# A vision-transformer layer on one core: where the odd group's attention weights are turned, where the even gates stand, and who issues the transfers that place the weights

## Chip, cores and metric

One core of one Trainium2 chip runs the whole kernel as a single program. The metric is the device time of one execution in microseconds (us). The kernel before has been timed three times; the median is given below.

## What is computed

64 images of 3x96x96 are cut into 36 patches of 16x16x3; each is multiplied to 256 features, a class token is put in front (37 tokens per image) and position vectors are added. Then follow one attention layer over the 37 tokens of each image (16 heads of 64) and one mixture-of-experts layer (8 experts, top 2, beside a shared one), each with a residual and a layer norm. The unusual part of attention is the position term, taken from a running sum of gates:

```python
sim = jnp.einsum('bid,bjd->bij', q, k) * scale
G = jax.nn.sigmoid(sim)
P = jnp.flip(jnp.cumsum(jnp.flip(G, axis=-1), axis=-1), axis=-1)
P = jnp.minimum(P, T_MAX - 1)
E = jnp.einsum('bnc,ct->bnt', q, pos_emb)
w = P - floor(P)
sim = sim + w * E[ceil(P)] + (1.0 - w) * E[floor(P)]
attn = jax.nn.softmax(sim, axis=-1)
out = jnp.einsum('bij,bjd->bid', attn, v)
```

All of it is in fp32.

## The kernel before

The work of the attention layer goes by **groups** of three images (111 rows, `ROWS`) and by **pairs** of groups. Group `g = 2p + a` is the even (`a = 0`) or odd (`a = 1`) group of pair `p`; there are 22 groups and 11 pairs, 0 to 10. The last group has one image and a packed form of its own. Pair 0 is written out (`first_pair` on TensorE and ScalarE), pairs 1 and 10 are written out too, and pairs 2 to 9 run in loops (on ScalarE 2 to 8, and 9 behind them). After attention come the shared expert, the router and the routed experts; the change doesn't touch them.

Nothing is scheduled by a tool: each engine's instructions stand in the order in which its block is written, and semaphores couple the engines. For one group the steps are these.

- `score(p, a)` on TensorE (L1010) gives scores and the products with the position table for all heads, in six PSUM banks `S`. VectorE copies the table part of an even group out (`tables_out`, L1985); ScalarE copies the scores out in three overlapping copies (L1494, L1496, L1498). ScalarE waits for VectorE's copy before it starts its own, and counts up `sim_sb` when the third is done. For an odd group ScalarE copies the table too (L1505).
- `values(p, a, s)` on TensorE (L1025, two products of 512 columns in four matmuls per two halves `k`) gives half `s` of the values in a bank of `X`; ScalarE's `values` (L1529) copies it out and counts up `v_ready`. Group `a = 1` uses the same two banks as `a = 0`, so TensorE's `values(p, 1, s)` waits until half `s` of the even group has been copied.
- ScalarE's `gates(p, a)` (tanh at L1514, then the gate at L1516) starts VectorE's long chain `cope`: the running sum `u` (L1908), its nearest even number and remainder (L1912, L1915), five bit masks (L1917), five predicated copies (L1925), the look-up (L1929 to L1942), and the logits (L1945 to L1949). In its midst (before L1933) it needs `qpos` from ScalarE's `distance` (L1523, L1524).
- ScalarE's `softmax_exp` (L1567) and VectorE's `softmax_norm` (L1969, L1971, L1975) give the attention weights `attn`.
- `turn_weights` on TensorE (L1047, eight transposes) turns them into two of the score banks. It waits for the next group's scores to be out of `S` (`sim_sb`, `table_sb`) and for the weights themselves (`attn_ready`). ScalarE's `weights` (L1535) copies them out, and six DMA transfers of 46 KB (`to_diagonal(j, b)`, two halves `j` by three images `b`) put the blocks on the diagonal of `attnT`. SyncE issues them (`place_attn`, L647). For group 0 and for groups 19 and 20, ScalarE issues the three of half `j = 1` behind its copies (L1546); `in_two_queues` says which.
- `outputs(g, a)` on TensorE (L1065) waits for all six (`placed`), and ScalarE copies the result to `oT` (L1559). `residual` (L1074) and `by_tokens` (L1090) finish a pair one pair later; `embed`, `keys` and `queries` (L921, L930) feed the next one.

In the loop, TensorE's order for pair `p` is: queries of `p` with the outputs of group `2p-2` between them, score of group `2p`, its two halves of values, **turn_weights of group 2p-1**, both halves of values of group `2p+1`, embed of the next pair, outputs of `2p-1`, score of `2p+1`, residual of the pair before, first keys, **turn_weights of group 2p**, keys, by_tokens. ScalarE's order from the scores on is:

```python
score(p, 0)
values(p, 0, 0)
values(p, 0, 1)
weights(p * 2 - 1, 1)
gates(p, 0)
split(p - 2)
distance(p * 2)
halves_of_x(p + 2)
outputs(p * 2 - 1, 1)
```

`split` prepares the normed rows of two pairs ago and `halves_of_x` the pixels of two pairs ahead. SyncE, in its own queue, goes through: store the hidden state, store normed rows, place the odd group (six issues), store halves, load pixels, turn pixels by a DMA transpose, place the even group (six issues), load the hidden state back.

Of the kernel before, what the change touches and what calls it, by code (L numbers as in the profile page):

```python
# [15 lines left out]
def vit_tower(nc, x, tok_w, tok_b, cls_token, pos_embed, wq, wkv, wout, b_out, cope_emb,  # L16
# [17 lines left out]
    TPG = 3  # L34
    ROWS = TPG * TOK
    G = -(-IMGS // TPG)
# [46 lines left out]
    with ExitStack() as ctx:  # L83
# [252 lines left out]
        o_done = sem("o_done")  # L336
# [108 lines left out]
        def to_diagonal(j, b):  # L445

            return (own_T[PAD * b:PAD * b + PAD, b, j * BLOCKS:j * BLOCKS + BLOCKS],
                    turned_attn[PAD * j:PAD * j + PAD, b])

        def in_two_queues(g):  # L450

            return isinstance(g, int) and (g == 0 or g >= G - 3)

        def slot_of(h):

# [16 lines left out]
        def next_first(p):  # L472
            return isinstance(p, int) and p == 1
# [50 lines left out]
        def apart(eng):  # L524

            eng.nop(nofuse=True)
# [56 lines left out]
        def _(sp):  # L583
# [52 lines left out]
            def place_attn(p, a):  # L636

                g = p * 2 + a
                if first(g):
                    sp.wait_ge(attnT_zeroed, 1)  # L640
                else:
                    sp.wait_ge(o_done, g * 2)
                sp.wait_ge(at_sb, g * 4 + 4)
                apart(sp)
                for j in range(2 - in_two_queues(g)):
                    for b in range(TPG):
                        sp.dma_start(*to_diagonal(j, b)).then_inc(placed[a], 16)  # L647

            def turn_x(p):

# [245 lines left out]
        def _(pe):  # L896
# [311 lines left out]
            def pair(p, ahead):  # L1208
# [8 lines left out]
                else:  # L1217
                    queries(p, ahead)
                    score(p, 0)
                    for s in range(2):  # L1220
                        values(p, 0, s)
                if ahead:
                    turn_weights(p * 2 - 1, True)
                    values(p, 1, 0)
                else:
                    values(p, 1, 0)
                    turn_weights(p * 2 - 1, True)
                    for c in range(2):
                        turn(c)
                values(p, 1, 1)  # L1230
# [228 lines left out]
        def _(act):  # L1459
# [66 lines left out]
            def values(p, a, s):  # L1526
                act.wait_ge(v_done, p * 4 + 2 * a + s + 1)
                keyed = keys_of(rows_of(p * 2 + a))
                nc.scalar.copy(v_sb[:keyed, a, 512 * s:512 * s + 512], X[:keyed, 1 - s]  # L1529
                               ).then_inc(v_ready, 1)  # L1530

            def weights(g, a):
                for j in range(2):
                    act.wait_ge(at_done, g * 4 + 2 * j + 2)
                    nc.scalar.copy(turned_attn[:2 * PAD, :, PER_BANK * j:PER_BANK * j + PER_BANK],  # L1535
                                   S[:2 * PAD, j, :PER_BANK * ROWS].rearrange("p (n b q) -> p b n q", n=PER_BANK, b=TPG)
                                   ).then_inc(at_sb, 2)

                if in_two_queues(g):
                    if g == 0:  # L1540
                        act.wait_ge(attnT_zeroed, 1)
                    else:
                        act.wait_ge(o_done, g * 2)
                    act.wait_ge(at_sb, g * 4 + 4)
                    for b in range(TPG):
                        act.dma_start(*to_diagonal(1, b)).then_inc(placed[a], 16)  # L1546

            def packed_weights(j):
                r = rows_of(G - 1)
# [13 lines left out]
            def softmax_exp(g):  # L1563
                act.wait_ge(logits, g + 1)
                r = lanes(g)
                n = heads(r)
                nc.scalar.activation(ex[:r, :n], lg[:r, :n], ACT.Exp).then_inc(exp_ready, 1)  # L1567
# [84 lines left out]
            def pair(p, ahead, ahead2):  # L1652
# [14 lines left out]
                values(p, 0, 0)  # L1667
                if not ahead:
                    softmax_exp(p * 2 - 1)
                values(p, 0, 1)  # L1670
                if ahead:
                    weights(p * 2 - 1, 1)
                if not next_first(p):
                    gates(p, 0)
                    split(p - 2)
                if ahead:
                    distance(p * 2)
# [812 lines left out]
```

## Time and profile before

| what | value |
|---|---|
| median of 3 runs | 717.65 us (717.54 to 722.87) |
| the profiled execution | 716.74 us |
| its span, first to last instruction | 715.0 us |
| TensorE busy | 683.1 us, 96% of the span |
| VectorE busy | 489.1 us, 68% |
| ScalarE busy | 422.9 us, 59% |
| chain that ended last | PE 44%, DVE 34%, issue 9%, ACT 7%, DMA 4% |
| mean granted clock of TensorE | 0.994 of full speed |

In profile rows PE is TensorE, PEld its weight loads, DVE VectorE, ACT ScalarE, POOL GpSimd, and SPq and ACTq are the sequencers of SyncE and ScalarE when they issue a transfer. A row of the timeline gives the start and the length of a run of like instructions in us. Neighbouring groups on one engine overlap a little (a group's length includes the emptying of the pipeline), so the next group can start 0.1 to 0.25 us before the length printed has run out. Idle time in brackets is counted from the printed end to the next start, with what ended it. TensorE's 96% hides small waits that come back once per pair.

### The profile page before, as it was taken

Reading aid. Unit: us, or ns where it says so; the run is one execution under the profiler, and the core shown is the slowest. Engines: PE = TensorE matmul, PEld = TensorE weight load, DVE = VectorE, ACT = ScalarE, POOL = GpSimd, SP = SyncE. Lnnn points to the kernel's source line nnn. Section 1 sums busy time; section 2 is a strip of 40 time slices with the busy share of each in tenths; the row PEclk is TensorE's granted clock in tenths of the full one; section 3 lists DMA queues with packets and bytes.
Section 4 is the critical chain, followed back from the end, with each engine's and each line's share of the span. In section 5 each row is a group of like instructions: output and inputs, shape, how many; then the busy total and the mean of one; then the engine's idle time right before and its main releaser. Section 6 shows DMA issues by size and latency. Waiting matters only on the chain.

```text
span 715.0 us, 14167 instructions
## 1 busy us (share of the span) xinstructions
PE 683.1 (96%) x4762; PEld 587.2 (82%) x4763; DVE 489.1 (68%) x1027; ACT 422.9 (59%) x730; POOL 123.0 (17%) x156
## 2 busy tenths in 40 slices
PE   8998999999999999999999999889999999999995
PEld 5897697978879696987969697658898999998884
DVE  3376787878978787897878789788962222332657
ACT  1563767576586657667675656544217777774453
POOL 2100000000000000000000000010014777775130
PEclk9999999999999999999999999999999999999998
DMA  9720321514132141414112103227304555552811
GB/s 274 224 66 16 77 60 35 95 47 103 49 80 74 36 94 48 99 54 94 43 41 58 47 18 104 85 88 237 128 15 108 146 138 131 145 130 57 286 69 54
DMA packets 81958, 67.16 MB, mean 94 GB/s; under 512 B 50646, under 2 KB 73196, under 8 KB 81928
## 3 DMA queue, kind: packets, MB, share of 16 engines
q1 hardware_dynamic: 76906, 56.30, 29.3%
q0 software_dynamic: 4224, 9.71, 4.5%
q10 hardware_dynamic: 798, 0.76, 0.3%
q8 instruction: 16, 0.26, 0.2%
q14 instruction: 14, 0.11, 0.1%
HBM read 35.60 MB, written 15.75 MB: 72 GB/s over the span
## 4 chain that ended last, share of the span: by engine, by line
PE 44%; DVE 34%; issue 9%; ACT 7%; DMA 4%; DVEq 1%; ACTq 0%; SPq 0%; POOLq 0%
PE ps_S L1419 11%; DVE table L1925 7%; PE ps_S L1150 7%; PE ps_S L1431 5%; PE ps_S L1352 3%; DVE u L1908 3%; DVE bit L1917 3%; PE ps_S L930 3%; PE ps_X L1025 2%; DVE nb L1937 2%; DVE nb L1940 2%; DVE mx L1947 2%; PE ps_X L1074 2%; DVE nb L1945 2%; PE ps_S L939 2%
## 5 line engine op out<-in xcount | busy, mean ns | idle before, releaser
L1419 PEld LDWEIGHTS ps_S<-attnT,v_sb 128*128 128x128 f32 x704 | 84.6, 192 | 4.6 <-ACT attnT L1772 2.1
L1419 PE MATMUL ps_S<-attnT,v_sb 128*128 128x128 f32 x704 | 85.8, 275 | 1.1 <-ACT attnT L1772 1.1
L1925 DVE COPY_PREDICATED table<-bit,table 111x112 f32<-111x112 int16 (+6 forms) x110 | 74.9, 681 | 11.2
L824 POOL TENSOR_TENSOR rs<-ve,neg_half 111x2 f32<-111x2 f32 x11 | 12.2, 1111 | 403.7 <-DVE ve L2011 403.7
L1025 PE MATMUL ps_X<-wkv_sb,hT 128*120 128x512 f32 (+1 forms) x176 | 81.3, 602 | 0.2 <-ACT v_sb L1529 0.2
L2356 DVE COPY attnT<-ps_S 128x256 f32<-128x256 f32 x44 | 18.7, 425 | 81.0 <-PE ps_S L1431 80.9
L1074 PE MATMUL ps_X<-oT,wout_sb 128*128 128x222 f32 x320 | 63.0, 354 | 0.0
L930 PE MATMUL ps_S<-hT,wq_sb 128*128 128x216 f32 (+1 forms) x320 | 61.6, 344 | 0.0
L1074 PEld LDWEIGHTS ps_X<-oT,wout_sb 128*128 128x128 f32 x320 | 59.3, 190 | 1.8 <-issue 1.8
L1025 PEld LDWEIGHTS ps_X<-wkv_sb,hT 128*120 128x120 f32 (+1 forms) x176 | 29.8, 181 | 35.0 <-issue 33.8
L930 PEld LDWEIGHTS ps_S<-hT,wq_sb 128*128 128x128 f32 x320 | 56.5, 188 | 1.3
L846 POOL DMA_INDIRECT attn<-hh_d,ids_x x44 | 45.2, 1027 | 59.2 <-issue 57.2
L1010 PE MATMUL ps_S<-kT,qT 64*111 64x150 f32 (+1 forms) x704 | 51.6, 297 | 3.0 <-ACT patT L1468 3.0
L1792 ACT COPY v_sb<-gu_sb 128x1024 f32 x44 | 45.7, 1039 | 13.6 <-issue 9.5
L1908 DVE TENSOR_TENSOR_SCAN u<-scan_keep,gate 111x624 f32<-111x624 f32 (+1 forms) x22 | 31.3, 1423 | 31.3 <-ACT gate L1516 31.3
L1010 PEld LDWEIGHTS ps_S<-kT,qT 64*111 64x111 f32 (+1 forms) x704 | 46.0, 173 | 8.0 <-ACT patT L1468 3.2
L860 POOL DMA_INDIRECT y_d<-attnT,ids_y x44 | 44.6, 1015 | 18.4 <-issue 12.2
L1431 PE MATMUL ps_S<-down_sb,q 128*128 x176 | 45.2, 380 | 0.4 <-DVE q L2350 0.4
L930 PE MATMUL ps_S<-hT,wkv_sb 128*128 128x216 f32 x232 | 44.9, 348 | 0.0
L921 PEld LDWEIGHTS ps_S<-patT,tokT 128*128 128x128 f32 x216 | 40.5, 188 | 4.4 <-issue 4.4
L1772 ACT COPY attnT<-table 128x512 int16<-128x512 int16 x44 | 33.7, 765 | 16.9 <-DMA table<-attn 16.9
L930 PEld LDWEIGHTS ps_S<-hT,wkv_sb 128*128 128x128 f32 x232 | 42.5, 188 | 0.0
(319 smaller groups left out, 1309.5 us busy)
## 6 DMA issues: line engine op xcount, KB each, us to landing
down_sb<-in_x_dram SPq DMA_DIRECT2D x10, 648.0 KB
attnT<-attn SPq DMA_DIRECT2D x117, 46.2 KB
gu_sb<-y_d SPq DMA_DIRECT2D x8, 512.0 KB, 6.6
h_d<-hT SPq DMA_DIRECT2D x11, 240.0 KB, 2.5
kept<-h_d SPq DMA_DIRECT2D x11, 240.0 KB, 2.8
h_d<-h SPq DMA_DIRECT2D x10, 222.0 KB
wkv_sb<-in_L_attn_Wkv_dram SPq DMA_DIRECT2D x2, 1024.0 KB, 12.2
gu_sb<-in_L_ffn_gate_w_dram SPq DMA_DIRECT2D x2, 1024.0 KB, 8.8
```

What stands on the lines that cost most here:

```text
L846: nc.gpsimd.indirect_dma_start(xg[:, b], None, hh_d[:, :], bass.IndirectOffsetOnAxis(ap=ids_x[:, t:t + 1], axis=0), bounds_check=REAL - 1, ...
L860: nc.gpsimd.indirect_dma_start(y_d[:, :], bass.IndirectOffsetOnAxis(ap=ids_y[:, t:t + 1], axis=0), y_sb[:, b], None, bounds_check=TOPK * R ...
L930: mm = nc.tensor.matmul(bank[:, i * NPAT:i * NPAT + n * (TOK - 1)], w[:, k, c:c + P], hT[:, k, :n, 1:TOK], start=(k == 0), stop=(k == KE - 1))
L1010: mm = nc.tensor.matmul(S[lane:lane + r, bank, col:col + KW], qT[part, f, a * ROWS:a * ROWS + r], kT[part, f, a], start=True, stop=True)
L1025: mm = nc.tensor.matmul(X[:keyed, 1 - s], hT[:, k].rearrange("p b t -> p (b t)")[:, at:at + keyed], wkv_sb[:, k, INNER + 512 * s:INNER + 5 ...
L1074: mm = nc.tensor.matmul(bank[:, m * COLS:m * COLS + w], wout_sb[:, f, m * P:(m + 1) * P], oT[:, f, :w], start=(f == 0), stop=(f == FT - 1))
L1150: mm = nc.tensor.matmul(bank_of(c, f)[:, j * CHUNK:j * CHUNK + w], sgu_sb[:, f // KE, k, j, lo:lo + P], h1T(c)[:, k, :w], start=(k == 0), ...
L1419: mm = nc.tensor.matmul(S[:, i, j * FF + f * P:j * FF + f * P + P], held[:, i, k, j, f * P:f * P + P], xgT[:, i, k], start=(k == 0), stop= ...
L1431: mm = nc.tensor.matmul(E[:, i, :EMB], hid[:, i, k * P:(k + 1) * P], down_sb[:, bass.ds(e, 1), k].rearrange("p o f -> p (o f)"), start=(k ...
L1792: nc.scalar.copy(held[:, i].rearrange("p k j f -> p (k j f)"), gu_sb[:, bass.ds(e, 1)].rearrange("p o k j f -> p (o k j f)")).then_inc(til ...
L1908: A.did(V.tensor_tensor_scan(flat(u, r)[:, ::-1], flat(scan_keep, r)[:, ::-1], flat(gate, r)[:, ::-1], 0.0, ALU.mult, ALU.add))
L1925: A.did(V.copy_predicated(near[:, :, :, 0:SL - d], by_side(bit[:, n], r)[:, :, :, 0:SL - d], near[:, :, :, d:SL]))
```

## The change

Three moves, none of which adds or removes arithmetic. In every pair from 1 to 9 TensorE turns the odd group's weights one value product later, behind `values(p, 1, 0)` instead of ahead of it (pair 10 already had that order). ScalarE's gates of the even group stand directly behind the copy of the first half of the values, ahead of the second half and of the turned weights, in pairs 2 to 10. And the split of the six placing transfers goes by `from_scalar`: for every odd group up to 17, ScalarE issues two of the six, and SyncE four; group 0 goes back to SyncE alone; groups 19 and 20 stay as they were.

```diff
-        def in_two_queues(g):
-
-            return isinstance(g, int) and (g == 0 or g >= G - 3)
+        def from_scalar(g, a):
+
+            if isinstance(g, int) and g >= G - 3:
+                return [(1, b) for b in range(TPG)]
+            return [(1, 1), (1, 2)] if a == 1 else []
...
                 apart(sp)
-                for j in range(2 - in_two_queues(g)):
+                for j in range(2):
                     for b in range(TPG):
-                        sp.dma_start(*to_diagonal(j, b)).then_inc(placed[a], 16)
+                        if (j, b) not in from_scalar(g, a):
+                            sp.dma_start(*to_diagonal(j, b)).then_inc(placed[a], 16)
...
-                if ahead:
-                    turn_weights(p * 2 - 1, True)
-                    values(p, 1, 0)
-                else:
-                    values(p, 1, 0)
-                    turn_weights(p * 2 - 1, True)
+                values(p, 1, 0)
+                turn_weights(p * 2 - 1, True)
+                if not ahead:
                     for c in range(2):
                         turn(c)
...
-                if in_two_queues(g):
-                    if g == 0:
-                        act.wait_ge(attnT_zeroed, 1)
-                    else:
-                        act.wait_ge(o_done, g * 2)
+                if from_scalar(g, a):
                     act.wait_ge(at_sb, g * 4 + 4)
-                    for b in range(TPG):
-                        act.dma_start(*to_diagonal(1, b)).then_inc(placed[a], 16)
+                    apart(act)
+                for j, b in from_scalar(g, a):
+                    act.dma_start(*to_diagonal(j, b)).then_inc(placed[a], 16)
...
                 if not ahead:
                     softmax_exp(p * 2 - 1)
+                if not next_first(p):
+                    gates(p, 0)
                 values(p, 0, 1)
                 if ahead:
                     weights(p * 2 - 1, 1)
                 if not next_first(p):
-                    gates(p, 0)
                     split(p - 2)
```

How the instructions stand on TensorE in the loop, from the even group's two halves of values on, in the program before (ISA and REGISTER_ALU are waits and the arithmetic for them; in brackets are the semaphores waited for):

```order
L1025 MATMUL ps_X<-wkv_sb,hT 120x512 x2
L1025 MATMUL ps_X<-wkv_sb,hT 120x512 [waits h1_ready]
L1025 MATMUL ps_X<-wkv_sb,hT 120x512
L1034 ISA
L1035 REGISTER_ALU [waits sim_sb]
L1044 ISA [waits table_sb]
L1047 MATMUL ps_S<-ident,attn 80x111 [waits attn_ready]
L1047 MATMUL ps_S<-ident,attn 80x111 x7
L1020 REGISTER_ALU
L1025 MATMUL ps_X<-wkv_sb,hT 120x512 [waits v_ready]
L1025 MATMUL ps_X<-wkv_sb,hT 120x512
```

And in the changed program (its lines are 3 higher from here on):

```order
L1028 MATMUL ps_X<-wkv_sb,hT 120x512 x2
L1028 MATMUL ps_X<-wkv_sb,hT 120x512 [waits h1_ready]
L1028 MATMUL ps_X<-wkv_sb,hT 120x512
L1023 REGISTER_ALU
L1028 MATMUL ps_X<-wkv_sb,hT 120x512 [waits v_ready]
L1028 MATMUL ps_X<-wkv_sb,hT 120x512
L1037 ISA
L1038 REGISTER_ALU [waits sim_sb]
L1047 ISA [waits table_sb]
L1050 MATMUL ps_S<-ident,attn 80x111 [waits attn_ready]
L1050 MATMUL ps_S<-ident,attn 80x111 x7
```

The first thing that TensorE waits for behind the even group's values was `sim_sb` and is now `v_ready`.

On ScalarE in the loop, from the last copy of the even scores on, before:

```order
L1498 COPY simS<-ps_S 37x666 [waits sim_part]
L1529 COPY v_sb<-ps_X 120x512 [waits v_done] x2
L1534 ISA
L1535 COPY attn<-ps_S 80x3x148 [waits at_done]
L1534 REGISTER_ALU
L1535 COPY attn<-ps_S 80x3x148 [waits at_done]
L1514 ACTIVATE th<-simS 111x592 [waits sim_sb]
L1516 ACTIVATE gate<-th 111x16x37 [waits tanh_sb]
L1589 ISA
L1591 ISA [waits h1_ready]
L1592 COPY pe_full<-h 111x512 [waits hh_stored_0]
```

and now:

```order
L1498 COPY simS<-ps_S 37x666 [waits sim_part]
L1529 COPY v_sb<-ps_X 120x512 [waits v_done]
L1514 ACTIVATE th<-simS 111x592 [waits sim_sb]
L1516 ACTIVATE gate<-th 111x16x37 [waits tanh_sb]
L1529 COPY v_sb<-ps_X 120x512 [waits v_done]
L1534 ISA
L1535 COPY attn<-ps_S 80x3x148 [waits at_done]
L1534 REGISTER_ALU
L1535 COPY attn<-ps_S 80x3x148 [waits at_done]
L1543 DMA attnT<-attn 40x296 [waits at_sb]
L1543 DMA attnT<-attn 40x296
```

One copy of values and two of turned weights no longer stand ahead of the gates, and two transfers stand behind the weights, ahead of `split` and `distance`.

On ScalarE ahead of pair 1, where group 0 is placed, before:

```order
L1535 COPY attn<-ps_S 80x3x148 [waits at_done] x2
L1546 DMA attnT<-attn 40x296 [waits at_sb,attnT_zeroed]
L1546 DMA attnT<-attn 40x296 x2
L1523 ACTIVATE qpos<-q 111x592 [waits q_ready]
L1524 ACTIVATE qabs<-q 111x592
L1468 COPY patT<-ps_S 128x432 [waits xt_done] x3
```

and now:

```order
L1535 COPY attn<-ps_S 80x3x148 [waits at_done] x2
L1523 ACTIVATE qpos<-q 111x592 [waits q_ready]
L1524 ACTIVATE qabs<-q 111x592
L1468 COPY patT<-ps_S 128x432 [waits xt_done] x3
L1564 ACTIVATE ex<-lg 111x592 [waits logits]
```

The three issues are gone from between the copies of the weights and `distance`.

## Rows read from the trace of the kernel before

**Rows 1.** Waits of TensorE, longest in total: us, times, longest us

```profile
PE ps_S L1047 <- DVE attn L1975: 5.3, 10, 0.9
PE ps_S L1047 <- ACT simS L1498: 5.2, 7, 0.8
```

**Rows 2.** Timeline of TensorE, one pair: start, length, line, [idle <-releaser]

```profile
277.21 3.69 PE L1025 MATMUL ps_X<-wkv_sb,hT 128*120 128x512 f32 x8
281.65 0.95 PE L1047 MATMUL ps_S<-ident,attn 111*80 111x111 f32 x8 [0.75 <-ACT simS L1498]
282.45 3.61 PE L1025 MATMUL ps_X<-wkv_sb,hT 128*120 128x512 f32 x8
285.89 4.67 PE L921 MATMUL ps_S<-patT,tokT 128*128 128x216 f32 x24
290.49 1.74 PE L1065 MATMUL ps_S<-attnT,v_sb 120*64 120x111 f32 x32
...
300.51 1.65 PE L930 MATMUL ps_X<-hT,wkv_sb 128*128 128x216 f32 x8
302.68 0.96 PE L1047 MATMUL ps_S<-ident,attn 111*80 111x111 f32 x8 [0.52 <-DVE attn L1975]
...
318.53 3.69 PE L1025 MATMUL ps_X<-wkv_sb,hT 128*120 128x512 f32 x8
```

**Rows 3.** Timeline of VectorE, the same pair

```profile
278.13 0.88 DVE L1985 COPY table<-ps_S 111x702 f32<-111x702 f32 x1
...
284.64 1.46 DVE L1908 TENSOR_TENSOR_SCAN u<-scan_keep,gate 111x624 f32<-111x624 f32 x1 [3.63 <-ACT gate L1516]
...
294.07 0.82 DVE L1933 COPY_PREDICATED nb<-qpos,table 111x592 f32<-111x592 int32 x1 [0.20 <-DVE nb L1929]
...
301.84 0.78 DVE L1975 TENSOR_TENSOR attn<-ex,rden 111x592 f32<-111x592 f32 x1 [0.20 <-DVE rden L1971]
```

**Rows 4.** Timeline of ScalarE, the same pair

```profile
281.33 1.06 ACT L1529 COPY v_sb<-ps_X 120x512 f32<-120x512 f32 x2
282.32 0.95 ACT L1535 COPY attn<-ps_S 80x444 f32<-80x444 f32 x2
283.17 0.70 ACT L1514 ACTIVATE th<-simS 111x592 f32<-111x592 f32 x1
...
287.50 0.70 ACT L1523 ACTIVATE qpos<-q 111x592 int32<-111x592 f32 x1 [1.86 <-DVE q L1915]
```

**Rows 5.** Timeline of SyncE's issues; then GB/s in 40 slices of 282 to 292 us

```profile
283.35 4.51 SPq L647 DMA_DIRECT2D attnT<-attn  x6
...
GB/s 0 0 0 0 0 0 0 0 0 0 19 152 19 5 166 19 5 166 19 14 175 0 14 175 0 9 180 21 61 49 45 41 61 37 29 66 53 61 70 74
```

**Rows 6.** Timelines of ScalarE, VectorE and TensorE, groups 0 to 2, 60 to 80 us

```profile
62.22 2.48 ACTq L1546 DMA_DIRECT2D attnT<-attn  x3
64.74 0.70 ACT L1523 ACTIVATE qpos<-q 111x592 int32<-111x592 f32 x1 [2.61 <-issue]
...
76.60 1.08 ACT L1529 COPY v_sb<-ps_X 120x512 f32<-120x512 f32 x2
...
65.53 0.82 DVE L1933 COPY_PREDICATED nb<-qpos,table 111x592 f32<-111x592 int32 x1 [6.14 <-ACT qpos L1523]
...
67.33 3.46 PE L1010 MATMUL ps_S<-kT,qT 64*111 64x150 f32 x32 [3.02 <-ACT patT L1468]
...
74.39 1.74 PE L1065 MATMUL ps_S<-attnT,v_sb 120*64 120x111 f32 x32 [1.22 <-ACT simS L1498]
...
77.25 3.69 PE L1025 MATMUL ps_X<-wkv_sb,hT 128*120 128x512 f32 x8 [0.23 <-ACT v_sb L1529]
```

**Rows 7.** Stretches: us, PE busy, PEclk, DMA share, GB/s

```profile
67.00:72.00 5.00, 4.67 (x34) 0.66 0.00 0
```

**Rows 8.** Timelines of ScalarE and TensorE, pair 10

```profile
448.01 2.29 ACTq L1546 DMA_DIRECT2D attnT<-attn  x3
...
453.88 1.75 PE L1065 MATMUL ps_S<-attnT,v_sb 120*64 120x111 f32 x32 [1.25 <-DMA attnT<-attn]
```

## The prediction

> **What bounds the kernel now.** I read the waits of TensorE first. Apart from one-off waits there are two that come back: the odd turn of weights waits for ScalarE's last copy of scores, 7 times for 5.2 us in all, and the even turn waits for VectorE's softmax, 10 times for 5.3 us [rows 1]. The reader is to see that TensorE, 96% busy, is not the bound of a pair; something else adds about 1.3 us to each.
>
> Then the timeline of one pair. Call T the start of its first value product, 277.21. The next pair's is at 318.53, so the period is 41.32 us [rows 2]. The eight value matmuls take 3.44 from start to start (282.45 to 285.89), so TensorE could go on at T+3.44 = 280.65 and does so at 281.65: the first wait costs 1.00 (0.75 in the row, the rest hides in the printed length). The eight key matmuls at 300.51 overlap their successor by some 0.16, so the even turn could start at 302.00 and starts at 302.68: 0.68. Without both the period would be 41.32 - 1.68 = 39.64.
>
> Then VectorE in the same pair [rows 3]. Its table copy starts at 278.13 = T+0.92 with no idle time before it, although the scores were done as the values began, some 0.1 after T. So VectorE is late, by 0.8, with the logits of the group before, and ScalarE waits for that copy before it reads the scores. This is a ring: table copy, score copies, two value copies, two weight copies, gates, running sum, ... logits, table copy. It has 41.32 us of work and waits of its own, and it is what bounds the pair; both waits of TensorE are its echo. The ring's only large gap on VectorE is the 3.63 before the running sum at 284.64, spent behind ScalarE's gates.
>
> **The gates, moved up (pairs 2 to 9).** From the first value copy (281.33) to tanh (283.17) ScalarE takes 1.84 [rows 4]: two value copies, 0.99 together, so 0.49 each, and two weight copies, 0.85. Now only one value copy stands between: 0.49. The ring gets 1.35 shorter, 39.97. That is less than any period that TensorE allows, so VectorE is no longer late: the table copy starts as soon as the scores are done, at about T+0.11 instead of T+0.92. The first value copy keeps its distance of 3.20 from it (278.13 to 281.33) and starts at T+3.31, tanh at T+3.80, the running sum 1.47 later (283.17 to 284.64 now) at T+5.27 instead of T+7.43. All of VectorE's even chain is 2.16 earlier.
>
> **The odd turn, moved back.** The wait for the scores goes, but a wait on a value copy takes its place: `values(p, 1, 0)` needs the bank that this copy empties. In pair 1 such a wait is seen: copy at 76.60, product at 77.25, 0.65 later [rows 6]. So TensorE goes on at T+3.31+0.65 = T+3.96, 0.52 later than it could, instead of 1.00. Bounds: 0 if the copy were never late, 1.33 if the table copy stayed where it is (T+4.12+0.65-3.44). I take 0.52, since the ring must be longer than TensorE's work for VectorE to stay late. Behind it, the turn at T+5.68 finds scores and weights long ready. The second value copy now stands behind the gates, starts at T+5.1 and is ready at T+5.8, while its bank is wanted at T+6.5, behind the turn.
>
> **The even turn.** TensorE reaches it at 302.00 = T+24.79, less 1.00, plus 0.52: T+24.31. The weights come at 302.68 = T+25.47 now and 2.16 earlier then: T+23.31. The 0.68 goes entirely, with 1.0 in hand. Per pair: 1.00 - 0.52 + 0.68 = **1.16**, period 40.16. What is late next is VectorE's ring, 0.19 below.
>
> **The transfers.** SyncE starts issuing 1.70 behind the start of the odd turn (281.65 to 283.35) and takes 0.75 for each [rows 2, 5]. The turn moves from T+4.44 to T+5.68, so issuing starts at T+7.38. Six would end at T+11.89, four end at T+10.39. The last transfer's burst of data (180 GB/s, slice 27, so 288.75) ends 0.9 after the last issue (287.86). The outputs want all six at T+13.28 - 0.48 = T+12.80: with six from SyncE the landing at T+12.79 has nothing in hand, with four it comes at T+11.3. So two issues moved just pay for the turn moved back. For ScalarE they are a cost: an issue takes it 0.84 (three from 62.22 to 64.74 [rows 6]), two 1.7, with a wait for its own copy in it. Queued behind are `split`, `distance`, the pixels and the copies of the outputs. Weights done at T+7.3, issues to T+9.1, `split` some 1.0 (gate end 284.6 to the start of the 1.86 idle), `distance` at T+10.2: it is at 287.50 = T+10.29 today, after 1.86 idle [rows 4]. The idle time and the copies moved forward pay for it, and all behind keeps its place. VectorE wants `qpos` at T+16.86 - 2.16 = T+14.70 [rows 3] and has it at T+11. I cost it at nothing; the cover is 3.7 us.
>
> A rule of the Trainium skill speaks against this edit: in "DMA: Bandwidth & Descriptors", section "Issuing engines are not separate DMA queues", it says that transfers of all issuers share the same 16 engines and interleave, so that a second issuer saves only sequencer time, usually small. The bursts of rows 5 come every 0.75 us with nearly nothing between them, so here the sequencer's time is what the landing waits for, and the saving is real. If bandwidth were the limit, the landing would stay at about T+12.8 and cost next to nothing more.
>
> **Group 0 back to SyncE.** ScalarE's three issues from 62.22 hold back `qpos` to 64.74, and VectorE stood idle 6.14 for it [rows 6]. Without them both go 2.6 earlier, and so does everything down to the outputs of group 0 (74.39) and the first value copy (76.60 to 74.0). TensorE's own wait of 3.02 at 67.33 shrinks too, but isn't the bound there. SyncE's six issues end at 62.2 + 4.5 = 66.7, well before 71.8. Here the turn moved back costs: no other work covers the value copy, so the product starts at 74.65, then 1.72, turn 0.80, 1.72: embed at 78.89 instead of 80.69 (77.25 + 3.44). Gain **1.8**; from there to pair 2 TensorE is dense and passes it on. Bounds: 2.6 above, 0 below if the clock falls (see below).
>
> **Pairs.** Pair 2: of the first kind of wait only 7 were seen, pairs 3 to 9; pair 2 had a hidden 0.25 and the 0.68: gain 0.4 against the 0.52, say **0.3**, since the gain builds up only once VectorE has caught up. Pairs 3 to 9: 7 x 1.16 = **8.1**; bounds 7 x 0.35 (a first wait of 1.33, second gone) = 2.5, and 7 x 1.35 = 9.4 (the ring's whole gain). Pair 10: TensorE waits 1.25 for transfers issued at 448.01 behind group 19's turn [rows 8]; VectorE comes less late into the pair, ScalarE's gates now stand ahead of the weights. Bounds 0 and 1.25; I take **0.5**. Behind pair 10 nothing is changed and all moves up.
>
> Sum: 1.8 + 0.3 + 8.1 + 0.5 = 10.7 us. The profiled execution took 716.74 (span 715.0 and 1.74 around it): 706.0. The median of the runs is 0.91 above it: **707.0**.
>
> **Rivals.**
> - *The clock falls in pair 1.* Today TensorE's gap of 3.02 at 67.33 is followed by a mean granted clock of 0.66 from 67 to 72 [rows 6, 7], that is, a part of these 5 us at the lower level of 1.2 GHz: 5 x 0.34 = 1.7 us of dense matmuls are lost, hidden behind VectorE. After the change the gap ahead of the outputs of group 0 is about 2.7 (69.0 to 71.8), then one of 1.2. If the clock falls after these, the 1.7 lies on the path: 708.7. For: a long gap with another behind it. Against: gaps of 1.2 alone did not do it.
> - *The new wait takes nearly all.* VectorE stays late for a reason not seen in the order, the table copy keeps T+0.92, and the first wait costs 1.33. Then 2.5 for pairs 3 to 9 and 2.6 for the rest: 717.65 - 5.1 = 712.5. Against it: the ring's sum.
> - *VectorE catches up wholly and value copies come sooner*: period 39.97, 7 x 0.19 = 1.3 less: 705.7.
> - *Slower: the transfers land late.* With two queues in pair 10 the last landing came 3.4 after the last issue (450.3 to 453.8), with large loads beside it [rows 8]. The outputs would then start at T+10.39+3.4 = T+13.8, 1.0 later than wanted: nearly all of the 1.16 is gone, about 715. With a landing of 4.5 each pair loses 2.1: 8 x (2.1 - 1.16) = 7.5 more than today, less 2.6 elsewhere: 722.6. It decides at 3.7. Against it: bursts of 0.9 in the loop and an empty stretch around them.
> - *The change doesn't do what it says*: not so; the order shows all three moves.
>
> **How the numbers follow.** Forecast 707.0: 0.50. Clock falls: 0.22. Ring limit 705.7: 0.08. New wait 712.5 or a mixture with the forecast: 0.15. Late landing: 0.05, of which 0.02 slower. About 1% (7.2 us, down to 710.5) is what a measurement of this kernel can tell from no change. The first three lie beyond it, and a part of the fourth: faster 0.84, same 0.13, slower 0.03. The range runs from 704.5 (ring limit and 1 us for the pieces at the ends) to 711.0, where part of the fourth is left out.
>
> **What would show it.** Right: period near 40.2; TensorE's wait on the scores replaced by one of about 0.3 in the rows on `v_sb` (L1025 by the old lines), seven or eight times; no waits on VectorE's `attn` in the loop; the table copy within 0.2 of T; `qpos` without idle time before it; no wait on `attnT<-attn` in the loop; embed of pair 1 near 78.9. Wrong: a `v_sb` wait of 1 us, an output product that waits for a DMA, a PEclk of 0.5 beyond 72 us, or VectorE waiting for `qpos`.

## Result, and the profile after

The changed kernel takes 707.33 us in the median of four runs (706.28 to 711.55); the kernel before, in the same comparison, 717.60 (717.36 to 722.87). The ratio is 0.9855, with a 95% interval of 0.9825 to 0.9884: faster by 1.2 to 1.8%. The forecast was 707.0. The profiled execution took 708.09 us (span 706.4, mean granted clock 0.995; before 716.74, 715.0 and 0.994). One more execution of the changed kernel, on another chip, took 723.92 us in a slower state, at a mean granted clock of 0.943; it is in no time and no ratio below.

The chain that ended last, by engine:

```profile
PE 81%; DVE 8%; ACT 6%; DMA 2%; issue 2%; ACTq 0%; DVEq 0%; SPq 0%; POOLq 0%
```

Before, TensorE had 44% of that chain and VectorE 34%: the path now runs mostly through TensorE itself. Of the kernels below, the three in which the gates keep their old place (the turn, the transfers and group 0, each alone) have 43 to 45% again, the others 74 to 90%.

**TensorE's waits.** The two that came back from pair to pair [rows 1] are gone. One took the place of the first; `attn` in L1050 remains once, in pair 10. The columns are those of rows 1.

```profile
PE ps_X L1028 <- ACT v_sb L1529: 3.2, 9, 1.1
PE ps_S L1068 <- ACT simS L1498: 2.5, 1, 2.5
...
PE ps_S L1050 <- DVE attn L1973: 0.9, 1, 0.9
```

Nine waits for the copy of the values: 1.12 in pair 1, 0.31 in pair 2, 0.26 in each of pairs 3 to 8 and 0.17 in pair 9. No wait names a transfer of `attnT`.

**TensorE, one pair**, to be laid beside [rows 2]. T, the start of the first value product, is 272.79 here. Where a view ends inside a run of matmuls, here and below, the count (x3 in the last row) and the length are those of the part shown; the start is not touched by it.

```profile
272.79 3.69 PE L1028 MATMUL ps_X<-wkv_sb,hT 128*120 128x512 f32 x8
276.74 1.98 PE L1028 MATMUL ps_X<-wkv_sb,hT 128*120 128x512 f32 x4 [0.26 <-ACT v_sb L1529]
278.55 0.93 PE L1050 MATMUL ps_S<-ident,attn 111*80 111x111 f32 x8
...
285.64 1.74 PE L1068 MATMUL ps_S<-attnT,v_sb 120*64 120x111 f32 x32
...
297.15 0.92 PE L1050 MATMUL ps_S<-ident,attn 111*80 111x111 f32 x8
...
312.96 1.55 PE L1028 MATMUL ps_X<-wkv_sb,hT 128*120 128x512 f32 x3
```

The period is 312.96 - 272.79 = 40.17 us (before 41.32). TensorE goes on at T+3.95, the odd turn is at T+5.76, the outputs start at T+12.85 without idle time, and the even turn at T+24.36 without idle time.

**VectorE, same pair** [rows 3]:

```profile
272.90 0.89 DVE L1983 COPY table<-ps_S 111x702 f32<-111x702 f32 x1
...
278.06 1.46 DVE L1906 TENSOR_TENSOR_SCAN u<-scan_keep,gate 111x624 f32<-111x624 f32 x1 [2.33 <-ACT gate L1516]
...
287.50 0.83 DVE L1931 COPY_PREDICATED nb<-qpos,table 111x592 f32<-111x592 int32 x1 [0.20 <-DVE nb L1927]
```

The table copy stands at T+0.11 (before T+0.92), the running sum at T+5.27 (before T+7.43). The 0.20 before L1931 is VectorE's own, not a wait for `qpos`.

**ScalarE, same pair** [rows 4], and the issues of SyncE beside it [rows 5]:

```profile
276.11 0.58 ACT L1529 COPY v_sb<-ps_X 120x512 f32<-120x512 f32 x1
276.59 0.70 ACT L1514 ACTIVATE th<-simS 111x592 f32<-111x592 f32 x1
...
280.22 1.49 ACTq L1543 DMA_DIRECT2D attnT<-attn  x2
281.91 0.62 ACT L1589 COPY pe_full<-h 111x512 int16<-111x512 int16 x1 [1.77 <-issue]
...
282.95 0.69 ACT L1523 ACTIVATE qpos<-q 111x592 int32<-111x592 f32 x1
```

```profile
280.21 3.15 SPq L650 DMA_DIRECT2D attnT<-attn  x4
```

One copy of values (0.48) now stands between the scores and tanh, where 1.84 stood. The two issues cost ScalarE 1.77; `qpos` starts at T+10.16, without idle time, where it was at T+10.29.

**Pair 1**, TensorE, to be laid beside [rows 6, 7]. The second fence is the granted clock of TensorE in two stretches (us, PE busy, PEclk, DMA share, GB/s).

```profile
71.46 3.23 PE L1068 MATMUL ps_S<-attnT,v_sb 120*64 120x111 f32 x32 [2.45 <-ACT simS L1498]
75.80 1.98 PE L1028 MATMUL ps_X<-wkv_sb,hT 128*120 128x512 f32 x4 [1.12 <-ACT v_sb L1529]
...
80.11 2.23 PE L924 MATMUL ps_S<-patT,tokT 128*128 128x216 f32 x11
```

```profile
68.00:72.00 4.00, 1.55 (x9) 0.89 0.00 0
72.00:76.00 4.00, 2.88 (x31) 0.68 0.00 0
```

The outputs of group 0 take 3.23 where the same 32 matmuls take 1.74 elsewhere: in this execution the clock was at the lower level (1.2 GHz) for part of that time. The embed comes at 80.11, forecast 78.89.

**Where the time went.** TensorE's first value product of pairs 2, 3 and 10, before and then after:

```profile
112.70 0.69 PE L1025 MATMUL ps_X<-wkv_sb,hT 128*120 128x512 f32 x1
...
153.28 0.69 PE L1025 MATMUL ps_X<-wkv_sb,hT 128*120 128x512 f32 x1
...
440.41 1.12 PE L1025 MATMUL ps_X<-wkv_sb,hT 128*120 128x512 f32 x2
```

```profile
112.03 1.55 PE L1028 MATMUL ps_X<-wkv_sb,hT 128*120 128x512 f32 x3
...
152.25 1.12 PE L1028 MATMUL ps_X<-wkv_sb,hT 128*120 128x512 f32 x2
...
431.44 1.12 PE L1028 MATMUL ps_X<-wkv_sb,hT 128*120 128x512 f32 x2
...
444.21 1.74 PE L1068 MATMUL ps_S<-attnT,v_sb 120*64 120x111 f32 x32 [1.54 <-ACT patT L1568]
...
530.96 1.27 PE L1419 MATMUL ps_S<-attnT,v_sb 128*128 128x128 f32 x9 [1.66 <-ACT attnT L1770]
```

| part | forecast | in the two profiled executions |
|---|---|---|
| pair 1 | 1.8 | 0.67 (112.70 - 112.03) |
| pair 2 | 0.3 | 0.36 (153.28 - 152.25 = 1.03, less 0.67) |
| pairs 3 to 9 | 8.1 | 7.94 (440.41 - 431.44 = 8.97, less 1.03) |
| pair 10 | 0.5 | 0.70 (453.88 [rows 8] - 444.21 = 9.67, less 8.97) |
| behind it | 0 | -1.03 (first expert product 539.60 before, 530.96 now: 8.64) |
| sum | 10.7 | 8.64 |

The last row of the fence is where 1.0 is given back: the first expert product waited 1.66 for ScalarE's `attnT` here and 0.63 before. In the chain that leads to it, ScalarE's copy waits for the DMA transpose `table<-attn`, and this took 4.25 here and 3.29 before, 0.96 of the 1.03.

### The profile page after: what moved, and what is told of

Its sections match the earlier page's. It is cut to its first block, busy times and chain, and to the rows that moved or that the text cites. A ratio compares the mean times of both kernels' runs of the same rounds, so it can differ in the third digit from the quotient of the medians.

```text
span 706.4 us, 14175 instructions
## 1 busy us (share of the span) xinstructions
PE 681.8 (97%) x4762; PEld 588.1 (83%) x4763; DVE 489.7 (69%) x1027; ACT 421.6 (60%) x730; POOL 122.8 (17%) x156
## 4 chain that ended last, share of the span: by engine, by line
PE 81%; DVE 8%; ACT 6%; DMA 2%; issue 2%; ACTq 0%; DVEq 0%; SPq 0%; POOLq 0%
PE ps_S L933 13%; PE ps_S L1419 11%; PE ps_X L1077 8%; PE ps_S L1153 7%; PE ps_S L1013 6%; PE ps_S L924 6%; PE ps_X L1028 6%; PE ps_S L1431 5%; PE ps_S L1068 5%; PE ps_S L1352 3%; PE ps_S L1050 2%; PE ps_X L933 2%; PE ps_S L942 2%; PE ps_X L1153 1%; DVE table L1983 1%
## 5 line engine op out<-in xcount | busy, mean ns | idle before, releaser
L1028 PE MATMUL ps_X<-wkv_sb,hT 128*120 128x512 f32 (+1 forms) x176 | 83.1, 604 | 3.2 <-ACT v_sb L1529 3.2
L1068 PE MATMUL ps_S<-attnT,v_sb 120*64 120x111 f32 (+1 forms) x704 | 39.2, 265 | 4.0 <-ACT simS L1498 2.5
```

What stands on the lines that cost most here:

```text
L1028: mm = nc.tensor.matmul(X[:keyed, 1 - s], hT[:, k].rearrange("p b t -> p (b t)")[:, at:at + keyed], wkv_sb[:, k, INNER + 512 * s:INNER + 5 ...
L1068: mm = nc.tensor.matmul(S[odd * DH:odd * DH + DH, 4 + half, f % 4 * ROWS:f % 4 * ROWS + r], v_sb[:keys_of(r), a, h * DH:h * DH + DH], weights,
```

## The experiments

Ten other kernels ran, and the changed one once more, each against the kernel before on its own chip. The ratio given with each is that of the comparison, with its 95% interval; it can lie up to 0.2% from the quotient of the two medians. Three questions: which of the three moves carries the gain; what each costs or saves in a pair; and why pair 1 gave 0.67 instead of 1.8. The theory is that of the prediction (the ring bounds the pair); its rivals were that the turn's move is what pays, or that the second queue does.

### The gates alone

The kernel before with only this:

```diff
                 values(p, 0, 0)
+                if not next_first(p):
+                    gates(p, 0)
                 values(p, 0, 1)
                 if ahead:
                     weights(p * 2 - 1, 1)
                 if not next_first(p):
-                    gates(p, 0)
                     split(p - 2)
```

> Only the gates are moved up; turn and transfers as before. Ring theory (the pair is bound by table copy, score copies, value and weight copies, gates, VectorE's chain): the ring gets 1.35 shorter, period 39.97 instead of 41.32, TensorE's wait for VectorE's softmax in the loop gone and its wait for the scores nearly so; nothing gained in pair 1. 7 x 1.35 + some 0.6 in pair 2 + 0.5 in pair 10: about 10.5 less than before, 707 us, as fast as the whole change. Rival (the moved turn brings about half of the gain, because it was TensorE that waited there): the gates alone bring the 0.68 of the second wait only, 7 x 0.68 = 4.8, about 712.5 us, period 40.64.

Measured: 707.53 us (706.41 to 711.73), before 717.65, ratio 0.9879 (0.9845 to 0.9913). TensorE, first rows of a pair, and VectorE's hand-over to the table copy:

```profile
272.30 3.69 PE L1025 MATMUL ps_X<-wkv_sb,hT 128*120 128x512 f32 x8
276.08 0.95 PE L1047 MATMUL ps_S<-ident,attn 111*80 111x111 f32 x8
```

```profile
271.87 0.78 DVE L1950 TENSOR_TENSOR lg<-nb,mx 111x592 f32<-111x592 f32 x1
272.56 0.88 DVE L1986 COPY table<-ps_S 111x702 f32<-111x702 f32 x1
```

The next pair starts at 312.26, so the period is 39.96; the ring was worked out as 39.97. The table copy starts at T+0.26, straight behind the logits, with the scores already done: the ring is still what bounds the pair, only 1.36 shorter. The turn starts at T+3.78 with no idle time printed, although eight value matmuls would let it start at T+3.44: a wait of 0.34 is hidden in the printed length. TensorE's own work of 39.64 and this 0.34 are again the period, to 0.02; it is so near to being the bound that the chain that ended last has 89% of TensorE. So the gates alone bring as much as the whole change (this median and that of the change are 0.2 apart).

### The turn alone, and the transfers alone

The kernel before with only the turn of the odd weights behind `values(p, 1, 0)`:

```diff
-                if ahead:
-                    turn_weights(p * 2 - 1, True)
-                    values(p, 1, 0)
-                else:
-                    values(p, 1, 0)
-                    turn_weights(p * 2 - 1, True)
+                values(p, 1, 0)
+                turn_weights(p * 2 - 1, True)
+                if not ahead:
```

> Only the odd turn is moved back; gates and transfers as before. Ring theory: ScalarE's gates stand behind the copies of the weights, which now wait for a value copy, a product (1.72) and the turn: 0.65 + 1.72 + 0.67 + 0.85 instead of 1.84 from the first value copy to tanh, so the ring gets 2.05 longer: period 43.4, 8 x 2.05 = 16 more, about 734 us, VectorE idle some 5.7 before its running sum. Rival (the turn's move earns): the first wait goes from 1.00 to at most 1.33, period 41.3 to 41.7, 717 to 720 us.

Measured: 737.23 us (735.76 to 740.00), ratio 1.0275 (1.0241 to 1.0308); the period is 43.41 (289.67 to 333.08). ScalarE in that pair shows why:

```profile
293.78 1.06 ACT L1526 COPY v_sb<-ps_X 120x512 f32<-120x512 f32 x2
296.86 0.95 ACT L1532 COPY attn<-ps_S 80x444 f32<-80x444 f32 x2 [2.02 <-PE ps_S L1047]
297.71 0.70 ACT L1511 ACTIVATE th<-simS 111x592 f32<-111x592 f32 x1
```

With the gates in their old place, the copy of the turned weights stands ahead of tanh and waits 2.02 for the later turn. Tanh starts 3.93 behind the first value copy instead of 1.84: the ring grows by 2.09, and 41.32 + 2.09 = 43.41.

TensorE also waits some 0.39 in each pair of the loop for a transfer of `attnT` ahead of the outputs, since all six are SyncE's here; the period shows no more than the 2.09 of the ring.

Then the kernel before with only the split of the transfers (the first, second and fourth hunks of the diff):

> Only the transfers as in the change: group 0 from SyncE, two of six of each odd group from ScalarE; gates and turn as before, so that the two issues stand ahead of the gates. Ring theory: the ring gets 1.75 longer (two issues and the wait for the own copy), period 43.1, 8 x 1.75 = 14 more, less 2.7 for group 0: about 729 us. Rival (issues cost ScalarE time that it has, and landings get earlier): 715 us, as group 0's part alone brings.

Measured: 729.48 us (727.75 to 731.43), ratio 1.0135 (1.0088 to 1.0182). Two even turns on TensorE, a period of 43.02, and ScalarE's tanh between them:

```profile
265.67 0.96 PE L1050 MATMUL ps_S<-ident,attn 111*80 111x111 f32 x8 [0.66 <-DVE attn L1975]
...
308.69 0.96 PE L1050 MATMUL ps_S<-ident,attn 111*80 111x111 f32 x8 [0.66 <-DVE attn L1975]
```

```profile
289.19 0.70 ACT L1517 ACTIVATE th<-simS 111x592 f32<-111x592 f32 x1 [1.61 <-issue]
```

Tanh starts 3.55 behind the first value copy (285.64), 1.71 more than the 1.84 before. Two issues ahead of the gates put the 1.7 into the ring: 41.32 + 1.70 = 43.02. Alone, both moves are losses. Behind the gates the same two issues cost nothing, while the moved turn stays a small loss (the turn back in its old place, below). Both rivals on which move pays have fallen.

### No issues from ScalarE

The changed kernel with six of six odd transfers issued by SyncE (group 0 included; groups 19 and 20 as before):

```diff
-            return [(1, 1), (1, 2)] if a == 1 else []
+            return []
```

> The whole change but for the two issues on ScalarE in the odd groups up to 17: SyncE issues all six, for group 0 too. Theory: the last transfer lands at T+12.8, when the outputs want it: a wait of 0 to 0.3 per pair, 707.3 to 709.5 us, period 40.17 to 40.45; ScalarE's chain has idle time before qpos again. Rival (issue time is hidden anyway, or the 16 engines set the landing): no wait at all, 707.3 as the change, the edit was for nothing. Second rival (ScalarE's issues held something back): faster than the change, under 706.

Measured: 713.16 us (712.56 to 713.92), ratio 0.9941 (0.9922 to 0.9959). More than expected. The issues, and what TensorE then waits for:

```profile
281.52 4.52 SPq L650 DMA_DIRECT2D attnT<-attn  x6
```

```profile
274.10 3.69 PE L1028 MATMUL ps_X<-wkv_sb,hT 128*120 128x512 f32 x8
...
287.42 1.74 PE L1068 MATMUL ps_S<-attnT,v_sb 120*64 120x111 f32 x32 [0.40 <-DMA attnT<-attn]
...
473.97 1.38 PE L1043 MATMUL ps_S<-ident,attn 101*37 101x101 f32 x8 [1.72 <-DVE attn L1961]
```

The last issue ends at 286.04 and the outputs start 1.38 later, at T+13.32, where they start at T+12.85 with four and two. The prediction had taken 0.9 for that last step, from where the burst of data ends, which is not yet where TensorE is released. 1.38 - 0.9 = 0.48, and the period is 40.64 (274.10 to 314.74) against 40.17: 0.47. Pairs 2 to 9 take 323.16 (first value products at 111.45 and 434.61) against 319.41 in the changed kernel, 3.75 more; with some 0.4 in pair 1 the six issues cost 4.2. The two profiled executions are 4.7 apart (712.77 and 708.09), and the rest is a balance of the clock: here it did not fall in pair 1 (1.5 less, see the filler below), but it fell behind the last row, the turn of the packed group. That takes 1.38 where it takes 0.86 in the changed kernel, at a granted clock of 0.74 from 475 to 480 us, and some 1.6 is lost from there to 479.28.

So the rule "Issuing engines are not separate DMA queues" of "DMA: Bandwidth & Descriptors" in the Trainium skill, which calls the sequencer time saved usually small, doesn't decide here. Between the first issue (281.52) and the moment at which the outputs would start without a wait (274.10 + 12.85 = 286.95) lie 5.43 us; less the 1.38, 4.05 are left for issuing, and six issues on one sequencer take 4.52. Two taken off it are worth 0.47 per pair.

### One issue from ScalarE

```diff
-            return [(1, 1), (1, 2)] if a == 1 else []
+            return [(1, 2)] if a == 1 else []
```

> The whole change, but ScalarE issues one transfer of the six of each odd group instead of two (SyncE five). From the run with six on SyncE: the last issue ended at T+11.94 and TensorE was let go 1.38 later, 0.47 after it could have gone on. Issue theory (the landing goes by SyncE's last issue, 0.75 each): with five it comes 0.75 earlier, just in time, no wait on attnT, period 40.17, within 1 us of the change (707.3). Rival (the landing goes by something that two issues on the second queue relieve, such as the rows' share of the 16 engines): a wait of 0.2 or more stays, 709 us.

Measured: 709.12 us (707.40 to 710.59), before 718.10, ratio 0.9856 (0.9815 to 0.9896). SyncE and TensorE:

```profile
280.29 3.81 SPq L650 DMA_DIRECT2D attnT<-attn  x5
```

```profile
272.86 3.69 PE L1028 MATMUL ps_X<-wkv_sb,hT 128*120 128x512 f32 x8
...
285.71 1.46 PE L1068 MATMUL ps_S<-attnT,v_sb 120*64 120x111 f32 x26
```

The fifth issue ends at T+11.24; plus 1.38 it is T+12.62, before T+12.85. No wait, and a period of 40.18. One issue would do; the second buys nothing that shows.

### The turn back in its old place

The changed kernel with the turn ahead of `values(p, 1, 0)` again, once without ScalarE's issues in the loop and once with them:

```diff
-                values(p, 1, 0)
-                turn_weights(p * 2 - 1, True)
-                if not ahead:
+                if ahead:
+                    turn_weights(p * 2 - 1, True)
+                    values(p, 1, 0)
+                else:
+                    values(p, 1, 0)
+                    turn_weights(p * 2 - 1, True)
```

Without (`from_scalar` returns an empty list for groups below 19):

> Gates up, group 0 from SyncE alone, but the odd turn in its old place ahead of the value product, and all other transfers from SyncE. Ring theory: TensorE's first wait is 3.63 - 3.44 = 0.19 instead of 0.52, the ring (39.97) binds: 7 x 0.2 less in pairs 3 to 9, and in pair 1 the turn covers the value copy again (0.8): about 2.3 less than the change, 705.0 us, faster than both kernels. Rival (the change's turn earns something): 708 us or more, with TensorE waiting for the scores 0.7 per pair again.

Measured: 704.66 us (703.40 to 704.79), ratio 0.9814 (0.9795 to 0.9832).

With them:

> The whole change with the odd turn back ahead of the value product; ScalarE still issues two transfers in each odd group. Against the version without these issues (704.7) it tells what they cost where nobody needs them. Theory (split and distance wait 1.7 more, VectorE has 3 us in hand for qpos): nothing, 704.4 to 705.2, period 39.97. Rival (the copies of the outputs behind the pixels come late and hold TensorE's scores up): 0.3 to 1 per pair, 707 to 712.

Measured: 704.36 us (703.21 to 705.25), before 720.01 in that comparison, ratio 0.9778 (0.9743 to 0.9812). TensorE, in the loop and in pair 1:

```profile
269.86 3.69 PE L1028 MATMUL ps_X<-wkv_sb,hT 128*120 128x512 f32 x8
...
309.83 1.55 PE L1028 MATMUL ps_X<-wkv_sb,hT 128*120 128x512 f32 x3
```

```profile
61.40 1.89 PE L1028 MATMUL ps_X<-wkv_sb,hT 128*120 128x512 f32 x4
...
73.45 0.96 PE L1050 MATMUL ps_S<-ident,attn 111*80 111x111 f32 x8
...
78.17 4.11 PE L924 MATMUL ps_S<-patT,tokT 128*128 128x216 f32 x21
```

The period is 39.97, and the two issues cost nothing: pairs 2 to 9 take 317.65 with them and 317.55 without. The two medians, from two chips, are 0.3 apart. Both versions are faster than the change and than the kernel before. What the moved turn costs: 0.20 per pair in the loop, 1.8 in pairs 2 to 9 (319.41 in the changed kernel), and in pair 1 the cover that the turn gives to the value copy, standing ahead of it as here at 73.45: from 61.40 to the embed at 78.17 it takes 16.77, against 17.54 with the turn moved and the clock at full speed (the filler, below), so 0.77. Together 2.5. The medians say the same: 704.4 here against 706.9 of the filler's kernel, on the same chip. One of the three moves is a loss of some 2.5 us inside a change that gains 10.

### Group 0 alone, and a filler in pair 1

The kernel before with group 0's six transfers from SyncE alone:

```diff
-            return isinstance(g, int) and (g == 0 or g >= G - 3)
+            return isinstance(g, int) and g >= G - 3
```

> The kernel before with one edit: SyncE issues all six transfers of group 0. Theory: qpos of group 1 comes 2.6 earlier, and so does the first value product of group 3; nothing in the loop changes, period 41.32: 2.7 less, 715.0 us. Rival (the ring absorbs it, since VectorE is late in the loop anyway): 717.6, since what pair 1 gains is waited away in pairs 2 and 3.

Measured: 716.42 us (714.78 to 718.41, ten runs), before 718.10, ratio 0.9960 (0.9934 to 0.9986). The medians give 1.7 gained, where 2.7 had been expected; the interval runs from 1.0 to 4.7, so it does not exclude that. In the profiled execution the clock fell behind the gap in pair 1:

```profile
72.01 3.23 PE L1065 MATMUL ps_S<-attnT,v_sb 120*64 120x111 f32 x32 [2.46 <-ACT simS L1498]
```

The first value product of pair 2 comes 0.90 earlier than before (111.80 for 112.70), and 0.81 of it is still there at pair 10 (439.60 for 440.41): the rival, by which the ring absorbs the gain, has fallen. In this execution it is lost again at the first expert product, which waits 1.62 instead of 0.63.

The filler is to keep TensorE at work there: in the changed kernel `values(1, 0, 1)` is computed twice, over itself, so that the gap shrinks from 2.45.

```diff
-                for k in range(KE):
+                for k in list(range(KE)) * (2 if next_first(p) and a == 0 and s == 1 else 1):
```

> The whole change, and in pair 1 the even group's second value product is computed twice (the second time over the first), so that TensorE's gap of 2.45 ahead of the outputs of group 0 shrinks to about 0.7. Clock theory (the change's scatter of 706.3 to 711.6 and the 1.2 us by which embed of pair 1 is later than worked out come from TensorE's clock falling behind that gap): PEclk 1.00 from 68 to 80, outputs of group 0 in 1.74 instead of 3.23, embed near 79, 1.2 to 1.5 us less in the runs in which the clock fell: median 706.2 or below. Rival (the clock falls for reasons outside this gap): no change, 707.3, or 1.7 more if the added product (1.7) were on the path.

Measured: 706.86 us (706.18 to 707.63, six runs), before 720.01, ratio 0.9811 (0.9777 to 0.9845). The median of 706.2 or below that was expected did not come, and the changed kernel was not timed on this chip, so what the filler is worth is read from rows alone. TensorE and its clock in two stretches:

```profile
61.57 1.89 PE L1028 MATMUL ps_X<-wkv_sb,hT 128*120 128x512 f32 x4
...
71.95 1.74 PE L1068 MATMUL ps_S<-attnT,v_sb 120*64 120x111 f32 x32 [0.74 <-ACT simS L1498]
...
79.11 3.17 PE L924 MATMUL ps_S<-patT,tokT 128*128 128x216 f32 x16
```

```profile
68.00:72.00 4.00, 3.26 (x10) 1.00 0.00 0
72.00:76.00 4.00, 2.88 (x35) 1.00 0.02 4
```

From the value product in front (61.57; 61.08 in the changed kernel) to the embed it takes 17.54 instead of 19.03: 1.49 less, all of it the outputs at 1.74 instead of 3.23. That is what the clock took from pair 1 in the changed kernel's profiled execution. Pair 2's first value product is at 111.03 here, 1.67 before the 112.70 of the kernel before: the forecast's 1.8 for pair 1, nearly whole once the clock stays up.

The filler together with the turn in its old place:

> The best version so far (gates up, group 0 from SyncE, turn in its old place, no issues on ScalarE in the loop), with the same doubled product in pair 1. Its profiled run showed no fallen clock there, so both theories say within 0.5 us of 704.7; the clock theory says that no run lies over 706.

Measured: 705.11 us (704.30 to 708.51, six runs), ratio 0.9798 (0.9761 to 0.9835), no faster than without it (704.66, on another chip). Its run of 708.51 had a mean clock of 0.990, the others 0.994 to 0.998: the clock also falls elsewhere, and the expectation that the scatter would end with the gap in pair 1 was wrong.

### The changed kernel once more

> The changed kernel itself, beside the other two on one chip, for its scatter. Clock theory: single runs between 706 and 712, each the later the lower its mean clock (0.998 about 706.5, 0.991 about 711.5). Rival: one value within 0.3%, 707.3, whatever the clock.

Measured on another chip, where the kernel before took 718.10: six runs from 705.98 to 710.55, median 709.3, beside the one of 723.92 named with the result; ratio 0.9856 (0.9821 to 0.9891), the first comparison's ratio again. The times go with the mean granted clock, though not strictly: 705.98 at 0.996, 707.11 at 0.998, the four from 709.10 to 710.55 at 0.990 to 0.993.

## Why the prediction was right, and where it was off

- **The ring bounds the pair**: right. Shorter by 1.35 it was to be 39.97; the gates alone give 39.96. Longer by the issues it is 43.02, by the late turn 43.41, in each case by just the time put in, and both were expected within 0.1 (43.1 and 43.4).
- **The gates, moved up**: right to the hundredth. Table copy forecast T+0.11, first value copy T+3.31, tanh T+3.80, running sum T+5.27; measured T+0.11, T+3.32, T+3.80, T+5.27.
- **The odd turn, moved back**: right in size (product at T+3.96, measured T+3.95), but its sign in the account was misleading. The step "1.00 - 0.52" books 0.48 as a gain of this move. But the gates alone take that wait from 1.00 to the hidden 0.34, and the move puts it up again to 0.51 (3.95 - 3.44): it costs 0.17 in this sum and 0.20 by the periods. The total was right since the whole was computed, not its parts.
- **The even turn**: the 0.68 went entirely, with T+24.36 for a forecast T+24.31. Period 40.17 for 40.16.
- **The transfers**: right that six from SyncE would be late by the turn's move and that ScalarE's issues cost nothing behind the gates (1.77 for a forecast 1.7, `qpos` at T+10.16 for T+10.2). Mis-sized was the term "ends 0.9 after the last issue": release comes 1.38 after it. Six from one queue thus don't land "with nothing in hand" but cost 0.47 per pair, 4.2 us in all. With four and two, if the same 1.38 holds, the landing is at 283.36 + 1.38 = T+11.95, 0.9 in hand instead of 1.5, so the time didn't suffer.
- **Group 0 back to SyncE, pair 1**: the mechanism was right. VectorE has `qpos` earlier and the outputs start at 71.46 for a forecast 71.8. The 1.8 became 0.67 in the profiled execution, since the first rival (the clock falls in pair 1) happened there: it priced 1.7 and the filler shows 1.49; with the clock up, pair 1 gains 1.67. The two runs at a clock of 0.998, 706.28 and 706.56, lie within 0.6 of the 706.0 that the sum gave.
- **Pairs 2 to 9**: 0.3 and 8.1, measured 0.36 and 7.94. **Pair 10**: 0.5, measured 0.70, but not where it was looked for, so this was luck. The wait ahead of the outputs, from which the 0.5 was taken, grew: 1.54 for ScalarE's `patT` where it was 1.25 for a transfer. The gain came ahead of it: the wait for the reload `wkv_sb<-h_d` (448.47 before, 438.51 now) fell from 1.29 to 0.60, and the turn's of 0.30 went. The prediction named neither.
- **"Behind pair 10 nothing is changed and all moves up"**: this step failed, by 1.0 in the two executions profiled. The wait at the first expert product isn't constant: 0.63 before, 1.66 after, 1.3 (the turn back in its old place) and 0.9 (one issue) in others. It goes with the DMA transpose `table<-attn` in front of it, which took 3.11 to 4.40 in the thirteen profiled executions, with waits of 0.60 to 1.82. The kernel with group 0 alone, whose loop and tail are those of the kernel before, waited 1.62, so the 1.0 can't be put down to the change. Why the transpose's time varies stays open.
- **The other rivals**: a new wait that takes nearly all (712.5), late transfers (715 or more) and the ring limit (705.7) didn't come; the ring's period of 39.97 is what one gets with the turn in its old place. The late transfers were mispriced: 1.0 of the 1.16 gone leaves 8 x 0.16 = 1.3 and the 2.6 from elsewhere, which is 713.8, not 715, and a pair breaks even at a landing of some 3.6, not 3.7.

The median met the forecast within 0.4 us, partly because two errors cancel. The profiled execution took 708.09 for a forecast 706.0, 2.1 more (10.7 forecast against 8.64). But the prediction put the median 0.91 above the profiled execution, as before, and it lies 0.76 below it: 1.67 back. That part is luck.

## What to carry to other kernels

When TensorE is 96% busy and still waits a little in every round, look for the loop through the other engines whose lengths add up to the period; shortening that loop by 1.35 moved the period by 1.35, and whatever else was put into it came back one to one. Price each move of a compound change in the kernel in which the others are already made: here the late turn looked like a saving of 0.48 and was a cost of 0.20 per pair, and it alone made the split transfers necessary. An issue cost its engine 0.75 to 0.9 us here, and was free only where what stood behind it had time in hand.

## What the runs showed of the hardware that was not expected

- **The same gap, two clocks.** Seven kernels have a gap of 2.45 or 2.46 on TensorE ahead of group 0's outputs, with the same work in front. In four profiled executions (the turn back in either form, the transfers alone, no issues from ScalarE) the clock stayed at 1.00 and the outputs took 1.74; in three (the changed kernel, one issue, group 0 alone) it fell, to 0.59 to 0.68 over 72 to 76 us. The gap alone doesn't decide; what does stays open. In the kernel with no issues from ScalarE it fell at 475 to 480 (0.74), behind a gap of 1.72; the changed kernel has a gap of 1.74 at that place and kept 1.00. With one issue it fell there too (0.62 from 470 to 475).
- **The scatter of one kernel's runs goes mostly with that clock.** The changed kernel's first four runs: 706.28 and 706.56 at 0.998, 708.09 at 0.995, 711.55 at 0.991. From 0.998 to 0.991 is 0.007 of some 706 us, 4.9 us, and the times differ by 5.3. The DMA transpose ahead of the experts, 3.11 to 4.40 in different executions, adds up to 1.2. With this, a difference of 2 us between kernels is only seen in medians of several runs, or in the starts of rows within a pair.
- **Landing and release.** With six small transfers in a row, the burst of data ends some 0.9 us after the last issue and the waiting matmul starts 1.38 after it (no issues from ScalarE; 1.37 with the turn alone, from 302.40 to 303.77). Half a microsecond per round hung on that.
